# A Flamingo block on one core: the K products among the sets of the second softmax, with three score banks instead of four

## The reference, cut to what matters

```python
def attention(query, key, value):            # 8 batches of 512 x 512, 16 heads of 32
    Q, K, V = query @ Wq.T + bq, key @ Wk.T + bk, value @ Wv.T + bv     # split into heads
    scores = Q @ K.T / sqrt(32)
    feats = [scores.mean(), scores.max(-1).mean(), softmax(scores).var(-1, ddof=1).mean()]   # per head
    t = exp(clip(mlp(feats), log 0.1, log 10))                                               # per head
    out = softmax(Q @ K.T / (2 * t)) @ V
    return out @ Wo.T + bo
x = x + tanh(g_xattn) * attention(layernorm(x), ctx, ctx)
x = x + tanh(g_ffn) * ffn(layernorm(x))      # w1, gelu, w2, weights ternary, activations 8 bit
```

## Time and profile before

| | us |
|---|---|
| median of 3 runs (1337.2 to 1338.84) | 1337.31 |
| the profiled execution | 1338.21 |
| its span, first to last instruction | 1336.3 |
| PE busy in the span | 1183.3 (89%) |
| DVE busy | 1097.7 (82%) |
| ACT busy | 936.5 (70%) |
| POOL busy | 394.2 (29%) |

### The profile page before, as it was taken

How to read it: one execution, slowest core, us unless ns; L and a number is a source line. 1 busy time by engine, 2 the same in 40 slices (tenths; PEclk the granted TensorE clock), 3 DMA queues, 4 the chain that set the end, 5 groups by cost and what they waited for, 6 DMA issues and landing times.

```text
span 1336.3 us, 23530 instructions
## 1 busy us (share of the span) xinstructions
PE 1183.3 (89%) x6684; PEld 438.0 (33%) x6684; DVE 1097.7 (82%) x2054; ACT 936.5 (70%) x1568; POOL 394.2 (29%) x387
## 2 busy tenths in 40 slices
PE   4856598989999999998999999998989899859988
PEld 2322221444124421444124432344214441224234
DVE  7789789896998869896998869897898979985256
ACT  4676599565985679575985669665885669765833
POOL 3148555311452024510353124510353101200120
PEclk9878789999999999999999999999999999979989
DMA  8712211221112221211112221112212210001000
GB/s 311 233 58 64 48 48 49 48 48 57 33 41 48 57 74 49 48 36 39 54 49 48 51 79 48 25 25 65 64 49 49 48 65 1 1 1 42 23 0 32
DMA packets 36049, 73.70 MB, mean 55 GB/s; under 512 B 8144, under 2 KB 8528, under 8 KB 35408
## 3 DMA queue, kind: packets, MB, share of 16 engines
q1 hardware_dynamic: 35920, 72.13, 18.9%
HBM read 38.39 MB, written 8.39 MB: 35 GB/s over the span
## 4 chain that ended last, share of the span: by engine, by line
PE 50%; DVE 26%; issue 10%; ACT 8%; SPq 3%; DMA 1%; DVEq 1%; POOL 1%; ACTq 0%; POOLq 0%
PE b_ps L1429 10%; DVE stat L1008 7%; PE o_ps L1669 6%; DVE nmax L998 5%; PE o_ps L1474 4%; PE o_ps L1429 4%; PE b_ps L1461 4%; ACT region L810 4%; PE a_ps L1455 4%; PE z_ps L1429 4%; ACT etile L778 3%; DVE hmax L1204 2%; PE z_ps L1669 2%; PE z_ps L1485 2%; PE b_ps L1634 2%
## 5 line engine op out<-in xcount | busy, mean ns | idle before, releaser
L778 ACT ACTIVATE etile<-a_ps,nmax 128x512 f32<-128x512 f32 x512 | 368.0, 732 | 113.8 <-DVE nmax L998 113.5
L810 ACT ACTIVATE region<-b_ps,inv2t 128x512 f32<-128x512 f32 x512 | 353.2, 754 | 49.9 <-PE b_ps L1461 45.8
L998 DVE TENSOR_REDUCE nmax<-a_ps 128x1 f32<-128x512 f32 x512 | 345.5, 677 | 51.7 <-PE a_ps L1455 48.1
L1008 DVE BATCH_NORM_STATS2 stat<-etile 128x6 f32<-128x512 f32 x500 | 339.8, 682 | 16.0 <-ACT etile L778 15.7
L1455 PE MATMUL a_ps<-kst,qst 96*128 96x512 f16 x512 | 198.8, 392 | 32.9 <-ACT etile L778 26.7
L1461 PE MATMUL b_ps<-qst,kst 97*128 97x512 f16 x512 | 193.0, 389 | 22.4 <-DVE region L1230 7.8
L1474 PE MATMUL o_ps<-region,vbuf 128*32 128x512 f32 x1024 | 137.3, 608 | 10.7 <-ACT region L810 7.0
L1485 PE MATMUL z_ps<-region,ones 128*32 128x512 f32 x1024 | 136.2, 604 | 9.5 <-DVE region L1040 9.5
L1461 PEld LDWEIGHTS b_ps<-qst,kst 97*128 97x128 f16 x512 | 49.3, 96 | 288.9 <-ACT region L810 258.1
L684 POOL TENSOR_TENSOR region<-region 128x512 f16<-128x512 f32 x64 | 77.0, 1203 | 210.9 <-ACT region L851 210.9
L640 POOL TENSOR_TENSOR region<-region 128x512 f32<-128x512 f32 x32 | 40.8, 1276 | 288.9 <-DVE region L1047 288.9
(11 more groups left out here) (312 smaller groups left out, 1977.8 us busy)
## 6 DMA issues: line engine op xcount, KB each, us to landing
kst<-region SPq DMA_DIRECT2D x96, 128.0 KB, 2.3
qst<-region SPq DMA_DIRECT2D x84, 128.0 KB, 2.3
xres<-in_x_dram SPq DMA_DIRECT2D x8, 1024.0 KB, 5.5
out_dram<-xres SPq DMA_DIRECT2D x32, 256.0 KB, 2.0
cin<-in_ctxT_dram SPq DMA_DIRECT2D x30, 256.0 KB, 2.7
cin<-in_x_dram SPq DMA_DIRECT2D x28, 256.0 KB, 2.6
kst<-in_f1T_dram SPq DMA_DIRECT2D x2, 1024.0 KB, 9.4
qst<-in_f2T_dram SPq DMA_DIRECT2D x2, 1024.0 KB, 9.0
```

What stands on the lines that cost most here:

```text
L778: nc.scalar.activation(etile[:, k % E_SLOTS, :], a_ps[k % A_BANKS][:, :], ACT.Exp, bias=nmax[:, slot_of(n), t:t + 1], scale=1.0, accum_out ...
L810: nc.scalar.activation(probs[:, (s + 1) % 2, g, :], b_ps[g % 2][:, :], ACT.Exp, scale=inv2t[:, slot:slot + 1]).then_inc(b_exp, 1)
L998: vec.tensor_reduce(nmax[:, slot_of(k // T), k % T:k % T + 1], a_ps[k % A_BANKS][:, :], AX.X, ALU.max, negate=True).then_inc(a_max, 1)
L1008: vec.bn_stats(stat[:, slot_of(k // T) * T + k % T, :], etile[:, k % E_SLOTS, :]).then_inc(a_stat, covered)
```

## The change

The K products of a steady iteration leave the projections. Each of the four is cut into two halves of six matmuls, run in sets 4 and 5, 7 and 8, 10 and 11, 13 and 14, as 2, 1, 2 and 1 matmuls behind the four places of a set. They go into the fourth A bank, so that A tiles of steady batches use three; ACT evicts each in the set that follows (6, 9, 12, 15), behind the B exponential of place 1. A POOL split moves with each. The sets take 44 A tiles instead of 40, the projections 20. The projections are then V0, V1 (three A tiles each), W (2, 2, 1, 1), X, Q0 to Q3 (two each), xq, V2; V3 stays behind up1. On DVE the normalisation and quantisation of the residual move from V's tiles to behind the tiles of Q0 and Q1, and `turned_xq` to behind those of Q3. Three A tiles instead of four are issued early.

```diff
-A_PLAN = (40, (2, 2, 2, 2, 1, 1, 1, 1, 1, 1, 1, 1, 2, 2, 2, 2))
+A_PLAN = (44, (3, 3, 0, 0, 2, 2, 1, 1, 0, 0, 0, 0, 2, 2, 2, 2))
...
-EARLY = A_BANKS
+EARLY = A_BANKS - 1
+K_PARTS = (2, 1, 2, 1)
+K_AT = {4: (0, 0), 5: (0, 1), 7: (1, 0), 8: (1, 1), 10: (2, 0), 11: (2, 1), 13: (3, 0), 14: (3, 1)}
+K_OUT_AT = {6: 0, 9: 1, 12: 2, 15: 3}
+def a_bank(b, k):
+    return k % (A_BANKS - 1 if steady_batch(b) else A_BANKS)
+def a_before(b, k):
+    if steady_batch(b):
+        return k + 1 - (A_BANKS - 1) if k >= A_BANKS - 1 else 0
+    return k + 1 - A_BANKS
...
+    if steady:
+        uses += some("X", T) + some("Q", C) + some("xq", T) + [("V", 2)]
...
@@ POOL, split_qk and body
+                    if has_b and n < C:
+                        pool_waits.wait_ge(k_free, nth(i + 1, C, n + 1))
+                        if n == C - 1:
+                            pool_waits.wait_ge(b_full, nth(i - 1, H * T, H * T))
...
+                if has_b and has_p:
+                    split_qk(0)
                     normalise_x(i + 1, 0, from_cin)
                     for n in range(2):
                         split_x(i + 1, n, from_cin)
                 if has_b:
                     split_y(i - 1, 1)
+                if has_b and has_p:
+                    split_qk(1)
+                    split_qk(2)
+                if has_b:
                     split_y(i - 1, 2)
+                if has_b and has_p:
                     normalise_x(i + 1, 1, from_cin)
+                    split_qk(3)
@@ ACT, body
                         if has_b:
                             second_exp(i - 1, s, g)
+                        if has_b and has_p and s in K_OUT_AT and g == 1:
+                            qk_out(K_OUT_AT[s], "K")
 
                         if has_a and g - 1 in set_tiles(i, s):
                             late_exp(i, set_tiles(i, s)[g - 1])
...
+                if has_b and has_p:
+                    v_out(range(2))
+                for t in range(T):
+                    tiles_a(C + t)
                 if has_p and not second:
                     x_out()
...
+                if has_b and has_p:
+                    for t in range(1, T, 2):
                         turned_xq(t)
+                    v_out((2,))
@@ DVE, body
+                    if has_b and has_p and n == 0:
+                        norm_residual(i - 1, c)
                     if has_b and has_p and n == 1:
-                        turned_xq(i)
+                        quantise_x(i - 1, c)
+                if has_b and has_p:
+                    turned_xq(i)
@@ PE
-                pe_waits.wait_ge(a_exp, nth(b, H * T, k + 1 - A_BANKS))
+                pe_waits.wait_ge(a_exp, nth(b, H * T, a_before(b, k)))
...
+                def k_part(n, half, g):
+                    if half == 0 and g == 0:
+                        if n == 0:
+                            pe_waits.wait_ge(c_done, nth(i + 1, C, C))
+                        pe_waits.wait_ge(k_free, nth(i + 1, C, n))
+                    cols = slice(n * P, (n + 1) * P)
+                    pairs = [(c, l, m) for c in range(C) for l, m in ((0, 0), (0, 1), (1, 0))]
+                    begin = half * len(pairs) // 2 + sum(K_PARTS[:g])
+                    for c, l, m in pairs[begin:begin + K_PARTS[g]]:
+                        ins = mat(k_ps[:, :], (w_hi, w_lo)[l]["k"][:, c, cols], (c_hi, c_lo)[m][:, c, :],
+                                  start=(c, l, m) == pairs[0], stop=(c, l, m) == pairs[-1])
+                    if half == 1 and g == G4 - 1:
+                        ins.then_inc(k_full, 1)
...
+                if steady:
+                    v_products(range(2))
+                    pe_waits.wait_ge(o_out, nth(i - 1, C, C))
+                    pe_waits.wait_ge(z_out, nth(i - 1, C, C))
+                    pe_waits.wait_ge(y_done, nth(i - 1, C, C))
...
                         drained(i, "X", t)
-                        if not first and (t < T - 1 or not has_b):
+                        if not first and (t < 2 or not has_b):
                             drained(i, "V", t)
...
+                if steady:
+                    for t in range(T):
+                        turned_xq(t)
+                    v_products((2,))
```

More of the change, by code:

```diff
@@ L145, in bank_uses @@
         uses += some("up0", NB, has_b) + some("up1", NB, has_b)
-    uses += some("V", T, has_p and setup is None)[T - 1:]
+    uses += some("V", T, steady)[T - 1:]
     for t in range(T):
@@ L180, in mm_use, with first_uses @@
     return n % MM, (i - 1) * (USES_ALL // MM) + n // MM
+def first_uses(i):
+    return list(USES[i if isinstance(i, int) and not 1 <= i <= 6 else 1])[:MM]
 def nth(b, per, k):
@@ L338, in flamingo_kernel @@
         o_ps, z_ps = bank("o_ps"), bank("z_ps")
+        k_ps = a_ps[A_BANKS - 1]
         mm_ps = b_ps + [o_ps, z_ps]
@@ L707, in body @@
                 for n in range(C):
-                    if has_p:
+                    if has_p and not has_b:
                         split_qk(n)
@@ L837, in tiles_a @@
                         late_exp(i, k)
[L839 to L852, removed]
                 if isinstance(i, int) and i == -1:
                     act_waits.wait_ge(bqk_in, 32)
-                for n in range(C):
+                for n in range(C) if not (has_b and has_p) else ():
                     tiles_a(n)
@@ L1317, in body @@
                     normalise(i - 1, C - 1, 1)
+                if has_b and has_p:
+                    normalise(i - 1, C - 1, 2)
                 for n in range(C):
                     tiles_a(n)
-                    if has_b and n == 0:
+                    if has_b and not has_p and n == 0:
                         normalise(i - 1, C - 1, 2)
@@ L1433, in split_product, with rested @@
                 ins.then_inc(mm_full[bank_n], 1)
-            def rested(i, has_p, banks):
-                for k in range(MM):
-                    if mm_ps[mm_use(i, "K" if has_p else "W", k)[0]] in banks:
-                        take(i, "K" if has_p else "W", k)
+            def rested(i, banks):
+                for stage, k in first_uses(i):
+                    if mm_ps[mm_use(i, stage, k)[0]] in banks:
+                        take(i, stage, k)
             def magnitude_sum(k):
@@ L1594, in turned_xq @@
                     ins.then_inc(mm_full[bank_n], 1)
+                if steady:
[3 more added lines that the diff above has]
+                    pe_waits.wait_ge(y_done, nth(i - 1, C, C))
+                for t in range(T) if has_p or not has_b else ():
+                    if has_b:
+                        split_product(take(i, "W", t),
+                                      [lambda c, l=l: yT[:, l, c, t * P:(t + 1) * P] for l in range(2)],
+                                      [lambda c, w=w: w["o"][:, c, :] for w in (w_hi, w_lo)], tiles_a(C + t), bias=1)
+                    else:
+                        alone(tiles_a(C + t))
                 if has_p and not second:
@@ L1599, in body @@
                     pe_waits.wait_ge(w_lo_done, 2)
-                else:
-                    v_products(range(T - 1) if has_b and has_p else range(T))
-                    if has_b and has_p:
-                        alone(tiles_a(C + 2 * T - 1))
+                elif not steady:
+                    v_products()
                 if second:
@@ L1657, in early @@
                         score_b(i, par, 0, g)
-                        if stages(i + 1)[0]:
+                        if stages(i + 1)[0] and g < EARLY:
                             score_a(i + 1, 1 - par, g)
```

100 lines of the change are left out of this document (53 added, 47 removed).

## The result

| | before | after |
|---|---|---|
| median, us | 1337.72 (1337.2 to 1338.84, 4 runs) | 1384.55 (1381.6 to 1388.61, 4 runs) |
| ratio | | 1.034, 95% interval 1.0314 to 1.0366 |
| span of the profiled execution | 1336.3 | 1385.4 |
| mean granted clock | 0.967 | 0.954 |

The change makes the kernel slower by 46.8 us, 7.8 us in each of the six steady iterations. The first view is the windows of one iteration of the changed kernel, cut at the same events as the earlier trace rows: sets 1 to 15; the projections in two pieces (the second from the third xq transpose to up0); up0, up1 and V3 until the first turn; the rest. Columns: stretch, length, busy time (x instructions) of PE, PEld, DVE, ACT and POOL, clock, DMA share, GB/s.

What follows compares the result with a forecast made beforehand. PE was taken as busiest in all four stretches, with ACT and DVE close in the sets. +11.2 - 4.8 - 0.65 - 1.6 = +4.2 us an iteration, six times +25 on 1338.2, gave 1363; range 1334 to 1388.

Steps and rivals of the forecast that it cites:

- three balanced engines in the sets: Sets 1 to 15 before: PE work 53.8 us, ACT 54.7, DVE 55, so three engines within 2 us of each other.
- three waits in the projections: PE idle 2.6 us between X and Q, 2.9 before Q3's second A score, 3.1 before the fourth xq transpose.
- wait for the context: First K part, set 4: PE waits about 1.3 us until POOL ends the last `c_lo`.
- evictions in sets 6, 9, 15: PE waits 0.85 us in each set for an A bank, since ACT evicts K before the exponential freeing it; 2.5 together.
- last exponential: End of the sets: PE waits 0.92 us for the last exponential, as in the kernel before.
- ACT needs 0.65 + 1.25 + 0.6 = 2.5: At an eviction: ACT's B exponential, K eviction and A exponential, against 1.7 us of PE work; 0.85 of wait.
- The rival at 1385: K sets: score, maximum, exponential and bank close a 5.05 us chain against PE's 5.02; 3.6 us more an iteration; chance 0.15.
- One bank for four K products: Sets: a whole set, 3.7 us, between products frees the bank in time; cost nothing, against 5 us an iteration by the skill.
- The rule on regimes: Skill: interleaving regimes with different most contended engines may improve time; cited for the faster rival, 1335 or 1317, chance 0.18.
- V2 (2.8) follows: End of the projections: V2 takes 2.8 us behind the fourth xq transpose's wait, and up0 starts at 45.7.
- The cover that V0 to V2 gave to the X copies: Between X and Q: V0 to V2 lay over ACT's 3.63 us of X copies; without them PE idles 2.6 us.
- The wait of 1.63 us: Feed-forward part: PE's wait before up2's fourth product, for DVE's `turned_h(0)`, goes; -1.6 us an iteration.

## Why the prediction was right in its direction and short in its size

The forecast was 1363, the result 1384.55: slower, inside the stated range of 1334 to 1388 but near its end, 22 us beyond the forecast and outside the 1347 to 1379 that it gave the forecast itself. The mechanism was the right one, three balanced engines in the sets and three waits in the projections; the terms had other sizes. A set's length is read from one `denominators` to the next; PE's own is by the paces of the earlier trace rows.

| us an iteration | forecast | measured |
|---|---|---|
| sets 1 to 3, no K part | +0.8 over PE's own | +1.5 (12.4 for 10.9) |
| wait for the context | 1.3 | 0.56 |
| evictions in sets 6, 9, 15 | 0.85 each | 1.46 each over PE's own 3.94 (3.72 and a K matmul) |
| eviction in set 12 | 0 | 0.8, at the start of set 13 |
| last exponential | 0.9 | 0.19 |
| sets 1 to 15 | +11.2 | +13.2 |
| projections | -4.8 | -2.5 |
| to the first turn | -0.65 | -0.67 |
| the rest | -1.6 | -2.2 |
| sum | +4.2 | +7.8 |

*Where the time went.* By the prediction's own counts PE's work grows by 11.7 us in the sets (53.8 to 65.5) and falls by 11.3 in the projections (48.4 to 37.1), so nearly the whole loss is time in which PE waits or runs slowly. In the sets that is 6.0 us before and 7.5 after (72.97 less 65.5); in the projections it is 2.0 before and 10.8 after (47.95 less 37.1), of which the three waits are 8.1 and V2's slow matmuls 1.5. The sets took in K at little more than its own price; it is the projections that didn't give the time back.

*The evictions.* The step that failed is "ACT needs 0.65 + 1.25 + 0.6 = 2.5" against PE's 1.7. It gives the wait at one A score and lets ACT arrive on time. By the whole set the rows already had most of the answer: 7 × 0.57 of the earlier trace rows and 1.25 of the earlier trace rows are 5.24 against the 3.72 of the earlier trace rows and one K matmul, 3.94, so 1.3 a set; the three sets took 5.40, 5.41 and 5.40. And the sum over the stage, ACT 62.6 against PE 65.5, hid this: ACT's work is thickest in the sets in which PE's is thinnest, and three A and two B banks let neither run far ahead, so the stage takes nearly the longer of the two set by set. The same count gives set 12 about 0.9: six exponentials and an eviction are 4.67 against the 3.73 that PE took; 0.8 of it appeared at the start of set 13. The prediction also opened with PE as the busiest engine in all four stretches; in the sets of the kernel before it is ACT, 56.65 us against 55.54.

*No lock step.* The rival at 1385 has the measured time and not the measured reason. It put its 3.6 us into K sets with DVE's extra work; the K sets 5, 7, 8, 10, 11 and 14, without an eviction, took 4.81 to 5.03 us, within 0.02 of PE's own, and the excess lies at the evictions. That a rival with another reason came nearest to the time was luck.

*One bank for four K products* was taken at nothing, and rightly: no K product in the changed kernel waits for it. Not following the rule quoted from the Trainium skill (Perfetto Trace Analysis, section Matmuls) did no harm here, because each eviction was over 1.8 to 2.7 us before the next product began; the split that held the bank longer showed its price, 1.13 to 1.53 us a product. The rule on regimes quoted from the Trainium skill (Perfetto Trace Analysis, section Optimization Strategy) had no gain behind it here: the sets rose by more than the projections fell.

*The projections.* The three waits came as forecast: 2.6, 2.9 and 3.1 became 2.69, 2.98 and 2.46. Up to the fourth xq transpose PE is 0.3 us behind the forecast (451.67 - 408.43 = 43.2 for 45.7 - 2.8 = 42.9). What failed is the last term, "V2 (2.8) follows": with up0 at 456.38 the transposes and V2 took 4.7. I had priced a wait at its length and not at what the clock does behind it; filling the waits showed 1.6 us an iteration of that. The cover that V0 to V2 gave to the X copies was named in the prediction and costed at 2.6; V2 alone put back was worth 3.0, its clock included.

*The feed-forward part.* The wait of 1.63 us is gone. Another 0.6 us went with it, and the two traces weren't followed to its cause.

## What to carry to other kernels

Where work moves beside other work, compare the engines' loads in the smallest stretch that the buffers can't bridge, here one set, and add up the longer of the two for each: equal sums over a stage say little. An eviction counts as work of the engine that makes it: reordering it moved most of the wait, while taking one out of the crowded stretch, with a later start of K, gave 10.6 us. A wait of the matrix engine costs its length and what the clock then takes from the matmuls behind it, so a product that needs nothing new belongs into the wait: V2 there was worth 18 us.

## What the runs showed of the hardware

The granted clock can fall inside a tuned iteration. Behind waits of 2.69, 2.98 and 2.46 us, with 10.8 and 2.4 us of matmuls between them, V2's matmuls came 0.43 us apart, the level of 1.2 GHz, and the clock was 0.77 over 7.5 us; with the same waits cut to 0.5 or 0.6 us by matmuls that nobody reads it stayed at 1.00. With only the first and the third filled it fell behind the second in three iterations of six. With the second at 1.90 us and the others open it still fell, for seven stretches in six iterations against ten in the changed kernel, though V2's matmuls were slow in only one of the six. The Trainium skill (Perfetto Trace Analysis, section Matmul Optimizations) says that TensorE scales its power with its use, so that matmuls should run back to back; these traces agree, and put 1.6 us an iteration on it.
